# Attention stage of a two-layer gated kernel: loads of row tiles and of P issued ahead of the weights, mask transposes between two output blocks, the gate columns computed after the masks

## The reference

```
x = x + tanh(g_xattn[0]) * L0_xattn(layernorm(x), ctx)
x = x + tanh(g_ffn[0])   * L0_ffn(layernorm(x))
x = x + tanh(g_xattn[1]) * L1_xattn(layernorm(x), ctx)
x = x + tanh(g_ffn[1])   * L1_ffn(layernorm(x))

L0_xattn:  q   = (h @ Wq.T) per head @ w_kc_q @ W_qr        # 16 heads, 64 wide
           kv  = rope(ctx);  k = kv @ W_kr                  # 128 keys per batch item
           P   = softmax(q k^T)
           out = ((P @ kv) @ w_kc_kv^T, all heads) @ Wo.T
L0_ffn:    probs = softmax(h @ Wr + br); w, idx = top_k(probs, 2)   # 8 experts
           combine = sum_k w_k * onehot(idx_k)
           a   = gelu(h @ W1 + b1 + lora1 of expert e)      # for the two chosen experts
           out = sum_e combine_e a_e @ W2 + combine.sum() * b2 + lora2
```

## Time and profile before

| | us |
|---|---|
| median of 3 runs | 1394.04 (1393.75 to 1394.27) |
| the profiled execution | 1391.57 |
| its span, first to last instruction | 1389.8 |
| PE busy | 1360.6 (98%) |
| DVE / ACT / POOL busy | 906.3 (65%) / 518.9 (37%) / 416.0 (30%) |
| mean granted TensorE clock | 0.996 of full speed |

### The profile page before, as it was taken

The page is one execution under the profiler, slowest core; times in us unless marked ns, Lnnn a source line. Parts: engine busy times, 40 slices in busy tenths (PEclk is TensorE's granted clock), DMA queues, the critical chain, the costliest instruction groups (busy, mean ns, idle before and its releaser), DMA issues.

```text
span 1389.8 us, 20437 instructions
## 1 busy us (share of the span) xinstructions
PE 1360.6 (98%) x7708; PEld 1103.3 (79%) x7708; DVE 906.3 (65%) x1759; ACT 518.9 (37%) x1569; POOL 416.0 (30%) x463
## 2 busy tenths in 40 slices
PE   7899999999999999999999999999999999999999
PEld 5688888888788788878887888788886788878887
DVE  5566565666674777786677657776888777834443
ACT  2444455454464232231113111311127777712221
POOL 3112423223254352111120111013518865530000
PEclk9999999999999999999999999999999999999999
DMA  7643444433444222110111101111224031131111
GB/s 264 185 153 114 149 124 129 144 107 119 154 147 111 80 76 57 54 38 20 31 46 31 42 23 45 36 46 56 80 82 137 33 114 62 58 116 57 53 46 46
DMA packets 86726, 120.51 MB, mean 87 GB/s; under 512 B 10444, under 2 KB 49484, under 8 KB 86628
## 3 DMA queue, kind: packets, MB, share of 16 engines
q1 hardware_dynamic: 86628, 119.21, 27.4%
HBM read 86.67 MB, written 32.51 MB: 86 GB/s over the span
## 4 chain that ended last, share of the span: by engine, by line
PE 88%; DVE 7%; ACT 2%; DMA 1%; issue 1%; POOL 1%; SPq 1%; DVEq 0%; ACTq 0%
PE bank L118 84%; PE bank L121 5%; DVE XR L140 1%; ACT Pb L124 1%; DVE STG L130 1%; DVE AH L130 1%; SPq L170 1%; DMA PYZ<-pscr 1%; DVE PYZ L164 0%; DVE XR L137 0%; DVE st L152 0%; ACT STG L124 0%; DVE sm L146 0%; DVE AH L127 0%; DMA XR<-in_x_dram 0%
## 5 line engine op out<-in xcount | busy, mean ns | idle before, releaser
L118 PE MATMUL bank<-XT,AR 128*128 128x512 f32 x1152 | 280.2, 393 | 0.3 <-DVE AR L130 0.2
L118 PE MATMUL bank<-AR 128*128 128x512 f32 x1056 | 262.3, 397 | 5.8 <-DVE Msb L127 4.9
L118 PEld LDWEIGHTS bank<-XT,AR 128*128 128x128 f32 x1152 | 213.8, 188 | 48.4 <-issue 1.5
L118 PEld LDWEIGHTS bank<-AR 128*128 128x128 f32 x1056 | 193.7, 188 | 52.2 <-DVE Msb L127 5.3
L124 ACT ACTIVATE STG<-bank,b1c 128x512 f32<-128x512 f32 x128 | 88.4, 690 | 379.1 <-PE bank L118 302.7
L118 PE MATMUL bank<-AR,CT 128*128 128x512 f32 x768 | 194.2, 396 | 1.8 <-DVE CT L130 1.8
L118 PE MATMUL bank<-AR,AH 128*128 128x512 f32 x768 | 187.6, 391 | 0.0
L127 DVE CAST AH<-STG 128x512 fp32r<-128x512 f32 x192 | 90.5, 471 | 120.9 <-PE bank L118 106.6
L118 PEld LDWEIGHTS bank<-AR,AH 128*128 128x128 f32 x768 | 143.0, 188 | 30.4 <-issue 1.1
L118 PEld LDWEIGHTS bank<-AR,CT 128*128 128x128 f32 x768 | 141.1, 190 | 30.1 <-DVE CT L130 2.5
L127 POOL CAST BA<-STG 128x256 fp32r<-128x256 f32 x64 | 29.7, 464 | 422.2 <-PE bank L118 321.1
(11 more groups left out here) (135 smaller groups left out, 1860.1 us busy)
## 6 DMA issues: line engine op xcount, KB each, us to landing
pscr<-PYZ SPq DMA_DIRECT2D x30, 512.0 KB, 2.9
PYZ<-pscr SPq DMA_DIRECT2D x120, 128.0 KB, 3.0
XR<-scr SPq DMA_DIRECT2D x52, 256.0 KB, 2.8
XR<-in_x_dram SPq DMA_DIRECT2D x32, 256.0 KB, 4.0
scr<-XR SPq DMA_DIRECT2D x32, 256.0 KB, 2.7
STG<-in_Wq_dram SPq DMA_DIRECT2D x8, 512.0 KB, 5.4
STG<-in_WoT_dram SPq DMA_DIRECT2D x8, 512.0 KB, 6.1
STG<-in_W1L_dram SPq DMA_DIRECT2D x16, 256.0 KB, 2.6
```

The costliest lines, as they stand in the source:

```text
L118: return self.e.matmul(o, w, x, start=start, stop=stop, skip_group_check=True) if self.e else Nothing()
```

## The change

In four places only the order of work is changed; no operation is added or dropped.

1. SP, steps 2 to 7 of the first stage: the row tiles (`ln_load`) and `p_load(u - 2)` are issued ahead of `prep_a(u + 2)` and `prep_b(u + 2)`. `prep_b(7)` loses its place of its own; it stands behind `prep_a(7)` in step 5, which is again behind `p_load(3)`.
2. TensorE, step 33: `mask_turn` moves from behind `wo1(31, (0, 1))` to between its two blocks.
3. DVE, `router_b`: the three instructions for the gate columns `w12c` and `w1c` move behind the last instruction of the masks. `tail_x` gets a wait for them.
4. DVE, steps 11, 19 and 27: `final1` of blocks 2 and 3 moves behind `pv1(u - 3)` and `ln_turn`.

```diff
 # tensor, step 33
                     stA0(0)
-                    wo1(31, (0, 1))
+                    wo1(31, (0,))
+                    mask_turn(0, 7)
+                    wo1(31, (1,))
                 if u == 34:
                     wo1(31, (2, 3))
-                if u == 33:
-                    mask_turn(0, 7)
 # vector, router_b
+            w1_at = {}
                 r1 = chain(e.recip(S(2), m8[:, :, 0]))
-                q2 = chain(e.tt(w12c[:, par, :], m8[:, :, 0], m8[:, :, 1], ALU.add))
                 iob = io8[:, :].unsqueeze(1).to_broadcast([128, 4, 8])
...
-                e.wait_ge(*q2)
-                chain(e.ts(w12c[:, par, :], w12c[:, par, :], tg[:, 1:2], None, ALU.mult, None))
-                chain(e.ts(w1c[:, par, :], m8[:, :, 0], tg[:, 1:2], None, ALU.mult, None))
...
                 e.tt(mB, mB, mA, ALU.subtract).then_inc(*ms_ok.mark(m))
+                q2 = chain(e.tt(w12c[:, par, :], m8[:, :, 0], m8[:, :, 1], ALU.add))
+                e.wait_ge(*q2)
+                chain(e.ts(w12c[:, par, :], w12c[:, par, :], tg[:, 1:2], None, ALU.mult, None))
+                w1_at[m] = chain(e.ts(w1c[:, par, :], m8[:, :, 0], tg[:, 1:2], None, ALU.mult, None))
 # vector, the loop over u
                     k1(u)
-                if 4 <= u < NU and (u - 4) % 8 == 7:
-                    final1((u - 4) // 8, 2)
-                    final1((u - 4) // 8, 3)
...
                     ln_turn(*after1(m), p - 3)
+                if 4 <= u < NU and (u - 4) % 8 == 7:
+                    final1((u - 4) // 8, 2)
+                    final1((u - 4) // 8, 3)
 # vector, tail_x
+                e.wait_ge(*w1_at[m])
 # sync, the loop over u
                 m, p = divmod(u, 8)
-                if u + 2 < 8:
-                    prep_a(u + 2)
-                if u + 2 < 7:
-                    prep_b(u + 2)
                 if u < NU and 2 <= p <= 4:
                     for tb in ((0,), (1, 2), (3,))[p - 2]:
                         ln_load(*after1(m), tb)
                 if 2 <= u < NU:
                     p_load(u - 2)
-                if u == 5:
-                    prep_b(7)
+                if u + 2 < 8:
+                    prep_a(u + 2)
+                    prep_b(u + 2)
```

## The result

| | before | after |
|---|---|---|
| median, us | 1393.74 (1391.31 to 1396.74, 20 runs) | 1388.41 (1386.68 to 1394.13, 20 runs) |
| the profiled execution | 1391.57 | 1387.11 |
| its span | 1389.8 | 1385.3 |

The ratio is 0.9966, with a 95% interval of 0.9957 to 0.9976: 4.7 us less. The two profiled executions differ by 4.5 us. I had forecast 10.2 us. The direction was right, the size less than half.

A forecast was written before the change was run, and what follows sets the result against it. PE, busy 98% of the span, bounds the kernel, so only its idles and low clock count. 5.8 + 1.4 + 3.0 = 10.2 us off the median gave 1383.9 us; range 1381.2 to 1388.6.

The forecast's parts named there:

- Part 1, what goes: First stage, step 3: PE's 4.90 us idle for Msb and 3.3 us of low clock behind it vanish.
- the 3.3 us: Step 3 behind the Msb wait: 5.92 us at half speed becomes 2.6 of work at full clock; 0.69 wait doesn't return.
- Part 1, the new wait: PE at prep_a(4), 48.7: a new wait of 2.4 us for Wqr, bounds 1.3 to 3.8.
- the clock stays up in the new wait: Wqr wait in step 3: full clock assumed, no cost; the rival, that it falls, cost 3.0 us (1386.9), chance 0.15.
- Later weights: First stage, steps 4 and 5: Wqr for prep_a(5) comes 2.7 us early; these steps cost nothing.
- late in every step: Rival, first stage: weights make PE wait again in step 4, 14.0 us slower, 1397.9; chance 0.04.
- Part 2: Steps 11, 19, 27: final1 behind pv1 ends PE's waits for CT, 1.4 us won, bounds 0 and 1.7.
- PE in step 12 asks for a bank that the exponentials free: Step behind the moved final1: later blends delay the exponentials; 0.1 us taken off for each of three steps.
- The waits for `CT` only change their name: Sign of error, steps 11, 19, 27: the forecast is wrong if other waits merely replace those for CT.
- Part 3: Masks: masks_a 1.3 us earlier, 12 matmuls behind it at full clock, 1.7 us; 3.0 us won, bounds 0 and 3.6.
- my 448.0: Sign in the changed profile: the mask transposes on PE start at 455.2 - 5.8 - 1.4 = 448.0.
- The masks' rival: Last mask instruction on DVE slips behind POOL's subtraction and is held: 3.0 us less won, 1386.9; chance 0.13.

The follow-up runs named there:

- the filling in the kernel before: Kernel before, with 17 additional matmuls of 128x512 into an unused bank between q1(3) and k1(3), result unread: 1393.12 us, ratio 0.9993.
- The filled version: Changed kernel, with 11 additional matmuls of 128x512 into an unused bank ahead of prep_a(4), result unread: 1385.91 us, ratio 0.9948.
- the two pairs: Changed kernel with 11 unread matmuls, final1 moved or at its old place: 1385.91, 1384.92 us; with P's load also ahead of row tiles: 1384.59, 1385.10.
- the version with P's load first everywhere: Changed kernel, weights one step earlier, P's load also ahead of row tiles in steps 11, 19, 27, final1's tiles later, B2T behind P's store: 1386.28 us.
- the version with only the loop mended: Changed kernel, P's load also ahead of row tiles in steps 11, 19, 27, final1's tiles one step later, B2T behind P's store: 1387.86 us.

## Why the prediction was right or wrong

**Part 1, what goes: right.** DVE was 4.8 us early by the forecast; its split began at 51.03 (forecast 51.1), `Msb` came at 54.2 (54), PE's waits for it and for the exponentials of step 2 vanished. With the clock kept up, step 3 gave 5.56 us against my 5.8, although `Wqr` was later than I had it. The size of the removed pieces was right in this surrounding. My working of the 3.3 us was nevertheless loose: I took the clock's share as 2.6 us of its own, and the filling in the kernel before gave 1.3 at most. That nearly all came back with DVE and ACT early too is what the two fillings, read together, suggest; no version separates it further.

**Part 1, the new wait: somewhat short.** 3.01 us, not 2.4, within my bounds of 1.3 to 3.8. `Wqr` took 4.7 us to land behind P's 512 KB and `kcqT`'s 384, where I had taken the 4.0 of a queue with as many bytes ahead. 0.6 us.

**Part 1, "the clock stays up in the new wait": this is the step that failed.** It fell at 49.8, some 1.5 us into a wait of 3.0, and stayed low for 10.2 us. The filled version puts its cost at 4.0 us, for which the sum had nothing. I had this as a rival, but with a chance of 0.15 and a price of 3.0 that I had copied from the 6 us of the kernel before. My only row for a clock that stays up, the idle of 2.38 us at 12.44, was misread. PE's timeline of the kernel before has, ahead of it and later:

```profile
7.27 2.79 PE L118 MATMUL bank<-STG 128*128 128x64 f32 x12 [7.27 <-DMA STG<-in_Wqr_dram]
...
68.19 0.60 PE L121 MATMUL bank<-ident,XR 128*128 128x128 f32 x4
```

The four transposes at 12.44 took 1.11 us, four of the same shape 0.60 at 68.19. The 12 matmuls at 7.27 took 2.79, as in the low stretch of the changed kernel, against 1.50 at 48.60. The windows print a clock of 1.00 there, but by these durations PE was at half speed on both sides of that idle, so no fall could show. What was left were the falls after 4.90 and after 2.01 us, and both spoke against me; "dense work of 1.5 us and more" on both sides had no row behind it. The work behind the new wait is 12 matmuls of 64 columns and 16 over 64 rows, and it ran at half speed like what followed up to 60.1. 5.8 - 0.6 - 4.0 = 1.2, measured 1.35.

**Later weights: right.** `Wqr` was issued again at 58.70 and `prep_a(5)` at 69.58 began without a wait, as did `prep_a(6)`. The rival "late in every step" didn't come.

**Part 2: wrong, 1.4 against nothing.** The three waits for `CT` went, and I had counted 0.1 each for what follows. For steps 11 and 19 that was near enough: 0.58 out, 0.18 in. But the gain is lost again in steps 28 to 30, as longer waits for ACT's exponentials: all in all 1.8 us out and 1.9 in when done alone, and 1.8 out and 1.8 or 1.7 in for the two pairs. The step that failed here is "PE in step 12 asks for a bank that the exponentials free", priced at 0.1 and for the next step alone. "The waits for `CT` only change their name" was my own mark of error; in the totals it came true.

**Part 3: right**, 2.86 against 3.0, and 3.1 by itself. The transposes came at 453.92; my 448.0 is off by 5.9 us, of which parts 1 and 2 failed to bring 5.7 by then. The masks' rival was real, as the version with P's load first everywhere shows: there 0.06 us decided. Its price was the idle, 1.2 us (1.89 against 0.45 + 0.23), without a fall of the clock.

**The sum.** 10.2 - 0.6 - 4.0 (clock) - 1.7 (part 2) - 0.1 (part 3) + 0.15 = 4.0, and 0.44 us of the profiled difference lie ahead of any change. The range ended at 1388.6 and held 1388.41, but by luck: it was wide enough for one mishap of 3.0 us, and two came (the clock, part 2), on a longer wait.

## What to carry to other kernels

A reordering that turns one wait into another must be priced at both: the new wait's own length, and whether the clock survives it, with all the matmuls that stand between it and the next point where another engine is late. Before a wait is counted as won, look for what ends second at the same place (here the exponentials behind `CT`), since that is what will be waited for. Before a row is taken as evidence that the clock stayed up, compare the durations of like matmuls in it. And if a wait can't be removed, it can be filled with matmuls that nobody reads: here that gave 4.0 us in the step, but 1.3 at most where PE then waited for ACT.

## What was not expected of the hardware

- The same kind of wait was followed by very different spells of low clock: 10.2 us after 3.01 us of idle in the changed kernel, and 6.8 us (52.8 to 59.7) after 2.95 us in the version with only the loop mended, where it fell 0.4 us after PE had started again, with the same matmuls behind. No fall came after 1.89 us of idle around the masks, although one had come there before after 0.62 and 1.39. What decides this is not settled.
- In the first 10 us of the old kernel's profile the windows print a granted clock of 1.00, while 12 matmuls of 128x64 took 2.79 us, against 1.50 later.
- A 128 x 4 instruction on DVE took 1.25 us beside a subtraction of POOL (1.33), and 128 x 32 took 1.25 when it began 0.06 us behind POOL's; 0.19 when both began within 0.01.
- A DMA of 192 KB landed in 4.7 us (forecast 4.0), and P's load could follow its store after 2.9 us in one order and after 5.4 in another, by what was in the queue.
- Executions of one kernel lie up to 7 us apart (1386.7 to 1394.1 for the changed one). The four of the changed one above 1392 have mean granted clocks of 0.995 or 0.996, its five fastest 0.996 to 0.998. Single profiles show the mechanism; the few us that they differ by need the medians.
